# Normalising chunks 1 to 3 of x with channels on partitions, and sending the row statistics over ScalarE's queue

## The reference

```python
lat = layer_norm(_layernorm(x), ln_lat_g, ln_lat_b)
ctx = layer_norm(context, ln_ctx_g, ln_ctx_b)
q = (lat @ Wq)                      # 512 -> 1024
k, v = jnp.split(ctx @ Wkv, 2, axis=-1)
k = apply_rope(k, cos, sin)
attn = softmax(clip(q @ k.T * scale, -11, 11))       # 16 heads of 64
x = x + tanh(g_xattn) * ((attn @ v) @ Wo + bo)
x = x + tanh(g_ffn) * int8_product(_layernorm(x), rhs)
```

## Time and profile before

| | us |
|---|---|
| median of 3 runs | 1479.47 (1477.96 to 1479.47) |
| the profiled execution, its own time | 1478.47 |
| its span | 1476.7 |
| TensorE busy in it | 1444.3 |
| VectorE busy in it | 1268.0 |
| ScalarE busy in it | 705.0 |
| mean granted TensorE clock | 0.99 |

### The profile page before, as it was taken

How to read it: one execution, slowest core, us unless ns; L and a number is a source line. 1 busy time by engine, 2 the same in 40 slices (tenths; PEclk the granted TensorE clock), 3 DMA queues, 4 the chain that set the end, 5 groups by cost and what they waited for, 6 DMA issues and landing times. The chain is left out here.

```text
span 1476.7 us, 22445 instructions
## 1 busy us (share of the span) xinstructions
PE 1444.3 (98%) x7938; PEld 872.4 (59%) x7938; DVE 1268.0 (86%) x1112; ACT 705.0 (48%) x821; POOL 101.8 (7%) x66
## 2 busy tenths in 40 slices
PE   8988999999999999999999999999999999999997
PEld 7866888888887444444444444444444444444774
DVE  6746878778774999999999999999999999996987
ACT  4422222222232665665656556565565656654342
POOL 0400000000000000000000000000000000001775
PEclk9998999999999999999999999999999999999998
DMA  8786777677667445541551551551452452403552
GB/s 278 262 240 234 258 261 225 223 249 239 242 196 248 113 102 185 137 109 44 136 127 26 135 128 32 133 127 38 122 128 47 111 128 56 103 16 94 156 165 86
DMA packets 156992, 219.22 MB, mean 148 GB/s; under 512 B 39697, under 2 KB 89873, under 8 KB 149777
## 3 DMA queue, kind: packets, MB, share of 16 engines
q1 hardware_dynamic: 153792, 213.35, 49.4%
q10 hardware_dynamic: 3152, 5.25, 1.0%
HBM read 133.70 MB, written 84.84 MB: 148 GB/s over the span
## 5 line engine op out<-in xcount | busy, mean ns | idle before, releaser
L1158 ACT ACTIVATE prob<-score_ps 128x1024 f32<-128x1024 f32 x512 | 483.0, 1032 | 198.7 <-PE score_ps L1105 198.7
L1117 PE MATMUL value_ps<-prob,v_st 128*64 128x512 f32 x2048 | 467.7, 598 | 1.0 <-DVE prob L1200 1.0
L1216 DVE TENSOR_TENSOR prob_sum<-prob_sum,prob 128x2048 f32<-128x2048 f32 x192 | 440.1, 2292 | 13.5
L1105 PE MATMUL score_ps<-q_st,k_st 64*128 64x512 f32 x3072 | 394.5, 402 | 2.2 <-PEq L112 2.1
L1105 PEld LDWEIGHTS score_ps<-q_st,k_st 64*128 64x128 f32 x3072 | 271.3, 184 | 173.7 <-issue 105.6
L1200 DVE TENSOR_SCALAR prob<-prob 128x4096 f32<-128x4096 f32 x128 | 292.6, 2286 | 41.3 <-ACT prob L1158 39.1
L1117 PEld LDWEIGHTS value_ps<-prob,v_st 128*64 128x64 f32 x2048 | 135.6, 136 | 267.6 <-issue 265.4
L873 DVE TENSOR_TENSOR k_cos<-k_raw,rope 128x1024 f32<-128x1024 f32 x32 | 39.2, 1224 | 64.3 <-ACT k_raw L702 64.3
L1525 POOL MEMSET unround<- 128x1 f32 x1 | 0.1, 98 | 1281.7 <-POOLq L122 1281.7
L702 ACT ACTIVATE k_raw<-proj_ps 128x1024 f32<-128x1024 f32 x31 | 31.9, 1029 | 111.9 <-PE proj_ps L245 111.9
L711 ACT ACTIVATE v_out<-proj_ps 128x1024 f32<-128x1024 f32 x31 | 31.9, 1030 | 110.5 <-PE proj_ps L245 110.5
(11 more groups left out here) (125 smaller groups left out, 1320.3 us busy)
## 6 DMA issues: line engine op xcount, KB each, us to landing
k_st<-k_scr SPq DMA_DIRECT2D x128, 256.0 KB, 6.2
k_scr<-k_hi SPq DMA_DIRECT2D x64, 256.0 KB, 2.9
v_scr<-v_out SPq DMA_DIRECT2D x32, 512.0 KB, 3.8
k_scr<-k_lo SPq DMA_DIRECT2D x64, 256.0 KB, 4.4
q_st<-q_scr SPq DMA_DIRECT2D x16, 1024.0 KB, 10.6
v_st<-v_scr SPq DMA_DIRECT2D x16, 1024.0 KB, 13.5
q_scr<-q_hi SPq DMA_DIRECT2D x32, 256.0 KB, 5.2
q_scr<-q_lo SPq DMA_DIRECT2D x32, 256.0 KB, 4.7
```

Source lines behind the costliest of these rows:

```text
L1105: last = pe.matmul(score_ps[:, u % BANKS, a, :], k_st[slot][rows, k_part, s * P:(s + 1) * P], q_st[slot][rows, q_part, cols], start=(t == ...
L1117: last = pe.matmul(value_ps[rows, :], v_st[slot][:, s, rows], prob[:, b % 2, i, a * CH:(a + 1) * CH], start=(s == 0), stop=(s == STEPS - 1))
L1158: act.activation(prob[:, b % 2, u % BATCH_UNITS, :], score_ps[:, u % BANKS, :, :], ACT.Exp, scale=SCALE).then_inc(exped, 1)
L1216: dve.tensor_tensor(total, total, halves[j], ALU.add).then_inc(added, 1)
```

## The change

Chunks 1 to 3 of x are now prepared like the context. A second copy of x with channels on partitions, `x_t`, is an input. Each of these chunks is loaded as rows for the statistics and from `x_t` as columns (`load_columns`) into storage that is free at the time: `k_lo` for chunks 1 and 3, `rope` for chunk 2. The transposes of these chunks, the normalisation of rows and the affine step out of `turn_ps` are gone; chunk 0 keeps them.

The statistics of chunks 1 to 3 and of context chunk 0 no longer go over SyncE. ScalarE stores them after its copy of m = 1 (`store_stats`), and after its copy of m = 2 it waits for the landing and issues the two broadcasts (`spread_stats`). During chunk n, all for chunk n + 1 (context chunk 0 counts as chunk 4): ScalarE takes the root after m = 0 and applies gain and bias after m = 4; VectorE inverts after m = 0, normalises after m = 3, splits after m = 5, and measures the chunk after that one after m = 7. `split_weight` stays at m = 4 and m = 6, behind the affine step. The scales of `rhs` are stored and loaded back by ScalarE, at (2, 4) and (2, 5).

From context chunk 1 on, only names and counts change. The core of the diff:

```diff
+    qtok = [rope[:, :, :, :].rearrange("p s f c -> p (s f) c"),
+            k_lo[:, :, :, :].bitcast(F32).rearrange("p s h c -> p (s h) c")]
+    def columns(n, slot):
+        return qtok[slot] if isinstance(n, int) and n < QCH else ctok[slot]
+    def loads(n, slot):
+        return n // 2 + slot
...
-        def load_chunk(n, slot, src):
-            if n >= 2:
-                sp.wait_ge(turned, KT * (n - 1))
-            sp.dma_start(raw[:, slot, :, :], src.rearrange("(t p) d -> p t d", p=P)).then_inc(raw_in[slot], 16)
-        def load_rows(c, tok0):
...
-                sp.wait_ge(ctx_moments_made, c)
-            sp.dma_start(raw[:, 0, :, :], context[bass.ds(tok0, CH), :].rearrange("(p t) d -> p t d", t=CT)
-                         ).then_inc(raw_in[0], 16)
-        def load_columns(c, slot, tok0):
-            if isinstance(c, int) and c < 2:
+        def load_rows(n, src, tok0):
+            slot = 1 if isinstance(n, int) and n == 1 else 0
+            if isinstance(n, int) and n == 2:
+                sp.wait_ge(turned, KT)
+            elif not (isinstance(n, int) and n == 1):
+                sp.wait_ge(moments_made, n - 1)
+            sp.dma_start(raw[:, slot, :, :], src[bass.ds(tok0, CH), :].rearrange("(p t) d -> p t d", t=CT)
+                         ).then_inc(raw_in[slot], 16)
+        def load_columns(n, slot, src, tok0):
+            if isinstance(n, int) and QCH <= n < QCH + 2:
                 sp.wait_ge(wkv_lo_made, KT)
-            else:
-                sp.wait_ge(tok_lo_made, QCH + c - 1)
-            sp.dma_start(ctok[slot], context_t[bass.ds(tok0, DIM), :].rearrange("(k p) c -> p k c", p=P)
+            elif not (isinstance(n, int) and n < 3):
+                sp.wait_ge(tok_lo_made, n - 1)
+            sp.dma_start(columns(n, slot), src[bass.ds(tok0, DIM), :].rearrange("(k p) c -> p k c", p=P)
                          ).then_inc(ctok_in[slot], 16)
...
-        def spread_stats(c, slot, row):
-            sp.wait_ge(ctx_rstd_made, c + 1)
+        def spread_stats(n, slot, row):
+            sp.wait_ge(rstd_made, n)
             sp.dma_start(stat_scr[bass.ds(row, 2), :].rearrange("f (p t) -> p f t", t=CT), stat[:, slot, :, :]).then_inc(stat_stored, 16)
-            sp.wait_ge(stat_stored, 16 * (c + 1))
-            if isinstance(c, int) and c == 0:
-                sp.wait_ge(tok_lo_made, QCH)
+            sp.wait_ge(stat_stored, 16 * n)
...
         def load_rope(c, slot, s0):
-            if not isinstance(c, int) or c >= 2:
+            if isinstance(c, int) and c < 2:
+                sp.wait_ge(tok_lo_made, 3)
...
-        def store_scales():
-            sp.wait_ge(rhs_inv_made, 1)
-            sp.dma_start(ready.scale_scr.rearrange("f (p t) -> p f t", t=KT), rhs_scales[:, :, :]
-                         ).then_inc(ready.scale_stored, 16)
-        def load_inverses():
-            sp.wait_ge(ready.scale_stored, 16)
-            sp.dma_start(inv_row[:, :], ready.scale_scr[1:2, :].broadcast_to((P, DIM))).then_inc(inv_row_in, 16)
         def load_piece(i, wo_row, rhs_row):
 
             if isinstance(i, int) and i == 0:
-                sp.wait_ge(turned, KT * QCH)
+                sp.wait_ge(moments_made, 1)
...
-        load_chunk(1, 1, chunk_rows(1))
+        load_rows(1, x, CH)
+        load_columns(1, 1, x_t, CH)
...
-                if m == 0 and n + 2 < QCH:
-                    load_chunk(n + 2, n % 2, chunk_rows(n + 2))
-                if m == 0 and n + 2 >= QCH:
-                    load_rows(n + 2 - QCH, (n + 2 - QCH) * CH)
+                if m == 0:
+                    load_rows(n + 2, *((x, (n + 2) * CH) if n + 2 < QCH else (context, (n + 2 - QCH) * CH)))
+                if (n, m) in ((0, 3), (1, 0)):
+                    load_columns(n + 2, n, x_t, (n + 2) * DIM)
                 if (n, m) in ((2, 5), (3, 1)):
-                    load_columns(n - 2, n - 2, (n - 2) * CH)
+                    load_columns(n + 2, n - 2, context_t, (n - 2) * DIM)
                 if (n, m) in ((0, 3), (1, 0), (1, 4), (2, 0)):
                     load_rhs_column((0, 1, 3)[n] + (m == 4))
-                if (n, m) == (2, 7):
-                    spread_stats(0, 0, 0)
-                if (n, m) == (2, 4):
-                    store_scales()
-                if (n, m) == (2, 6):
-                    load_inverses()
...
+        def sqrt(n, slot):
             twice = isinstance(n, int) and n < QCH
-            act.wait_ge(meanvar_made, turns_before(n, part) + 1)
-            act.activation(std[:, tiles], meanvar[:, tiles, 1], ACT.Sqrt, bias=(eps_sq if twice else eps_col)[:, 0:1],
+            act.wait_ge(meanvar_made, n)
+            act.activation(std[:, :], stat[:, slot, 1, :], ACT.Sqrt, bias=(eps_sq if twice else eps_col)[:, 0:1],
                            scale=1.0 + EPS if twice else 1.0).then_inc(std_made, 1)
...
+        def affine(n, slot):
             which = 0 if isinstance(n, int) and n < QCH else 2
-            if not isinstance(n, int) or n >= 1:
-                act.wait_ge(tok_lo_made, n)
+            tile = columns(n, slot)
+            act.wait_ge(scaled, n)
             for k in range(KT):
-                act.wait_ge(turned, KT * n + k + 1)
-                act.activation(tok[:, k, :], turn_ps[:, k, :], ACT.Identity, bias=gains[:, which + 1, k:k + 1],
+                act.activation(tile[:, k, :], tile[:, k, :], ACT.Identity, bias=gains[:, which + 1, k:k + 1],
                                scale=gains[:, which, k:k + 1]).then_inc(affine_made, 1)
 
-        def sqrt_rows(c, slot):
-            act.wait_ge(ctx_aggregated, c + 1)
-            act.activation(std[:, :], stat[:, slot, 1, :], ACT.Sqrt, bias=eps_col[:, 0:1]).then_inc(ctx_std_made, 1)
-        def affine_columns(c, slot):
-            act.wait_ge(scaled, c + 1)
-            for k in range(KT):
-                act.activation(ctok[slot][:, k, :], ctok[slot][:, k, :], ACT.Identity, bias=gains[:, 3, k:k + 1],
-                               scale=gains[:, 2, k:k + 1]).then_inc(affine_made, 1)
+        def store_scales():
+            act.wait_ge(rhs_inv_made, 1)
+            act.dma_start(ready.scale_scr.rearrange("f (p t) -> p f t", t=KT), rhs_scales[:, :, :]
+                          ).then_inc(ready.scale_stored, 16)
+        def load_inverses():
+            act.wait_ge(ready.scale_stored, 16)
+            act.dma_start(inv_row[:, :], ready.scale_scr[1:2, :].broadcast_to((P, DIM))).then_inc(inv_row_in, 16)
+        def store_stats(n):
+            act.wait_ge(rstd_made, n)
+            act.dma_start(stat_scr[2 * n:2 * n + 2, :].rearrange("f (p t) -> p f t", t=CT), stat[:, n % 2, :, :]
+                          ).then_inc(stat_stored, 16)
+        def spread_stats(n):
+            act.wait_ge(stat_stored, 16 * n)
+            act.wait_ge(tok_lo_made, 1)
+            for f in range(2):
+                act.dma_start(rows[:, n % 2, f, :], stat_scr[2 * n + f:2 * n + f + 1, :].broadcast_to((P, CH))
+                              ).then_inc(rows_in[n % 2], 16)
...
-                if (n, m) == (0, 0):
-                    sqrt(1)
-                if m == 6 and n + 2 < QCH:
-                    sqrt(n + 2)
-                if m == 6 and n + 2 == QCH:
-                    sqrt_rows(0, 0)
-                if m == (4 if n == 0 else 3) and n + 1 < QCH:
-                    affine(n + 1)
-                if m == 3 and n + 1 == QCH:
-                    affine_columns(0, 0)
-                if m == 5 and n + 1 == QCH:
+                if m == 0:
+                    sqrt(n + 1, (n + 1) % 2)
+                if m == 1:
+                    store_stats(n + 1)
+                if m == 2:
+                    spread_stats(n + 1)
+                if m == 4:
+                    affine(n + 1, (n + 1) % 2)
+                if (n, m) == (2, 4):
+                    store_scales()
+                if (n, m) == (2, 5):
+                    load_inverses()
+                if (n, m) == (3, 5):
                     wo_high(0)
...
-        def measure_rows(c, slot):
-            dve.wait_ge(raw_in[0], 16 * (c + QCH // 2))
-            for t in range(CT):
-                last = dve.bn_stats(moments[:, t, :], raw[:, 0, t, :])
-            last.then_inc(ctx_moments_made, 1)
-            if not (isinstance(c, int) and c < 2):
-                dve.wait_ge(stat_stored, 16 * (c - 1))
-            dve.wait_ge(ctx_moments_made, c + 1)
+            if not (isinstance(n, int) and n < 3):
+                dve.wait_ge(stat_stored, 16 * (n - 2))
+            dve.wait_ge(moments_made, n)
             dve.memset(spacer[:, :], 0.0)
             for t in range(CT):
                 last = dve.bn_aggr(stat[:, slot, :, t], moments[:, t, :])
-            last.then_inc(ctx_aggregated, 1)
...
-        def invert_rows(c, slot):
-            dve.wait_ge(ctx_std_made, c + 1)
-            dve.reciprocal(stat[:, slot, 1, :], std[:, :]).then_inc(ctx_rstd_made, 1)
-        def normalise_columns(c, slot):
+            last.then_inc(meanvar_made, 1)
```

(90 more changed lines are left out.)

71 lines of the change are left out of this document (30 added, 41 removed).

## The result

The changed kernel takes 1521.59 us (median of 5 runs, 1520.55 to 1523.66) against 1478.87 before: a ratio of 1.0296, with an interval from 1.0282 to 1.0309. It is 43 us slower. I had forecast 1501 in a range of 1485 to 1518. The profiled execution took 1523.66 us, its span is 1521.8.

What follows compares the result with a forecast made beforehand. TensorE, busy 98% of the span, was taken as the bound: new stops 36.6 and clock 8.6, less 22.6 won, make 22.4 us on the profiled 1478.5, so 1501 us, range 1485 to 1518.

Steps and rivals of the forecast that it cites:

- The 22.6 us to be won: Ceiling on TensorE: 17.3 us from stops of 8.68 and 3.94 with slow groups, 5.3 from three sets of transposes.
- N: Start of VectorE's subtraction for the next chunk; TensorE can start that chunk at N + 10.1, or N + 19.9 if held twice.
- GpSimd's hold: Chunks 0 and 1: GpSimd's 4.64 us subtractions delay VectorE's two casts twice, N + 19.9 in place of N + 11.9; chance 0.5.
- Rival 1: GpSimd holds VectorE's casts once, not twice: 4.64 us less in each of two chunks, 1492 us; not held, 1485; chance 0.22.
- The row at 41.27: Old kernel's VectorE: one L746 TENSOR_SCALAR took 4.92 us, median 0.54, over GpSimd's subtraction; taken as the hold's price.
- the column of rhs in chunk 1: Issued about 61.3, landing 72.2, ahead of VectorE's normalising; N = 73.5, a 17.0 us stop, VectorE's wait near 9.
- The trip: Statistics from ScalarE's store to VectorE's first use: 8.8 us, 3.0 for the store and 5.8 for the broadcasts.
- I take 3.0 us: Landing time assumed for the statistics' 4 KB store on ScalarE's queue; bounds 3.0 and 8.2 us.
- rival 2: ScalarE's queue gives no shorter trip, 14.1 us stays; 19 us more, 1520; chance 0.15.
- the extra loads: 3 MB of x_t and 1.5 MB of broadcasts, 12 us of DMA time at 379 GB/s, priced at nothing.
- the clock: TensorE's slow first group after a stop: 2.6 us after each long stop, 1.7 after each short one, 8.6 together.
- the mark: When TensorE is full again in the context's first product: 129.45 us before, forecast 151.9, 22.4 us more.

Runs made afterwards that it cites:

- run 1: The changed kernel with GpSimd made to wait for VectorE's tok_lo before its low parts of the k and v weights: 1505.97 us.
- run 2: The changed kernel with its 1 MB loads issued behind the statistics' round trip, rows after m = 4 and columns after m = 5: 1511.0 us.
- run 3: The changed kernel with the statistics stored and spread by SyncE again, behind its stores of m = 1, in place of ScalarE: 1526.51 us.
- run 4: The kernel before, with only the statistics of context chunk 0 stored and spread by ScalarE in place of SyncE: 1477.04 us, ratio 0.9999.
- Run 5: The changed kernel plus an unneeded 2 MB store on SyncE at (2, 0), 0.1 us ahead of the statistics: 1523.41 us in one run.

## Why the prediction was right and wrong

**Right: the sign, the place and the number of stops.** The 22.6 us to be won were won (the two old stops with their slow groups, and the transposes) and are outweighed by one stop per chunk. After the start of the subtraction, N, the chain is as worked out: N + 19.6 in chunk 0 (36.14 to 55.71, forecast 19.9), N + 19.5 in chunk 1 (77.04 to 96.58), N + 10.1 in chunk 2 (117.33 to 127.47, forecast 10.1).

**Right: GpSimd's hold, twice in each of two chunks.** Casts of 8.92 and 8.91 us in place of 1.28; run 1 takes it away and wins 15.6 us, 14.3 of them in these two stops. Rival 1, held once, is refuted. The row at 41.27 was not quite the one exception before: GpSimd's other subtraction there, at 36.01, took 5.67 us in place of 4.64 beside `tok_lo` (34.88 to 37.17), which also reads two operands from SBUF.

**Right: the column of rhs in chunk 1.** It landed in 10.2 us and held VectorE 8.06, forecast 10.9 and near 9. The stop there, 16.39, was forecast as 17.0. The trip, 13.3 us at most, lay under it, but only just, as run 2 shows; so a part of this hit is luck. Two small errors cancel as well: SyncE issued the column 9.95 us after the chunk's start where I had 9.2 (and the items that I named for it add up to 7.9 only), and it landed 0.7 sooner than forecast.

**Wrong: "I take 3.0 us, the later stores' value, since ScalarE's queue holds little else".** This is the step that failed. The store took 7.0, 6.7 and 9.6 us in chunks 0, 2 and 3, and the trip was not 8.8 but 12.8, 12.6 and 19.9 us. The 5.8 us of the broadcasts held in chunks 0 and 2 (5.8 and 6.0) and failed in chunk 3 alone (10.2, from 145.13 to 155.34). That is my rival 2, to which I gave 0.15: the queue gives no shorter trip. Runs 3, 4 and 5 show it: on SyncE's queue the trips are hardly longer or shorter, the queue alone gains nothing, and 2 MB more on the other queue make the trip 5.4 us longer. That the rival's 1520 comes within 1.6 us of the median is luck in part: it had 14.1 us for each trip, two were shorter and one was 5.8 longer, and it did not have the `q_lo` below.

The row that spoke for the rival stood in my own list: 8.2 us for 4 KB at 93.48. The 3.0 came from the context stage, and I did not ask what the DMA share is there: 0.55 over such a trip, and 0.76 over the one at 93.48. Nor is the share enough to price it: in chunk 1 of the changed kernel the store landed after 3.1 us at a share of 0.93, while only 129 GB/s moved; in the other three chunks it was 288 to 301 GB/s. And I did not see what runs 3 and 4 show, that SyncE, freed of the wait, sends its next 1 MB into the trip: 19.9 us for 13.4, and 17.9 for 14.1.

The Trainium skill ("DMA: Bandwidth & Descriptors", the section on issuing engines that are not separate DMA queues) says that transfers run on the same 16 engines and interleave, whoever issues them, and that only issuing time is saved. Runs 3 and 4 agree (4.9 us more, and a ratio of 0.9999). Run 5 agrees in that the other queue's 2 MB count, but the 4 KB landed 1 us behind them.

**Costed at nothing: the extra loads. Not shown to be wrong.** I wrote that they were 12 us of DMA time, and "without the stops as cover they would lengthen the trips". The engines were full in the trips: over the four of the changed kernel the windows view has a DMA share of 0.99, 0.92, 0.97 and 0.97. But little of that is `x_t`. Its first load had landed at 19.0 us, ahead of all trips; the second was issued at 33.85, 2.3 us before the trip of chunk 0 ended; the third, at 65.18, lies in chunk 1, where it was counted with the column. In the trips of chunks 2 and 3 there are rows and columns of the context, tables and stores of q, which the kernel before moves as well. What is new is where they lie. Run 2 moves all 1 MB loads, old and new, and so doesn't tell the extra ones apart.

**Missed: what the context's first product waits for.** Its row says `q_lo`, not `tok_hi`. VectorE makes the `q_lo` of m = 6 behind `tok_lo` (165.37 and 167.57 above), so the stop ends at N + 13.2 (155.34 to 168.51) and not at N + 10.1: 3.1 us more.

**Mis-sized: the clock.** I had 1.7 us for each of two stops of 3.15, and they became 6.50 and 16.75. Also the shorter of them was followed by a slow group of 5.1 us; the four groups cost 9.5 in place of 8.6.

The account, measured less forecast: chunk 0 3.2 (16.55 for 13.3), chunk 1 -0.6, chunk 2 3.3, chunk 3 13.6 (16.75 for 3.15: the trip 11.1, `q_lo` 3.1, and 0.6 less elsewhere), clock 0.9. That is 20.4 of the 21.7 us by which the mark lies later than forecast (173.54 for 151.9); the rest is a late start of 0.2 and small pauses at the stops. For chunk 3, run 3 gives a part of the answer to what made the trip long: with nothing issued behind the store until 154.35 it took 13.4 us, 7.6 for the store and 5.8 for the broadcasts, so the traffic issued behind it is worth up to 6.5 of the 19.9. Run 5 varies what is ahead. How the engines order the two is not settled.

## What to carry to other kernels

A round trip through memory for a few KB took 9 to 20 us here, by what the DMA engines had to move meanwhile, whatever queue issued it. Take its price from a stretch where as many bytes are under way, and not from the share alone; start it ahead of the next large load, and see what the engine that used to wait for it will issue instead. When work moves within a hand-written order, look for what the other engines do at its new place: here GpSimd's subtractions had cost TensorE nothing for as long as no cast lay beside them. Replacing 5.3 us of transposes on the full engine by a chain over three engines and the memory pays only if the whole chain fits into the time between two chunks.

## What the runs showed of the hardware

Two things beyond what I had expected. A store of 4 KB, alone on ScalarE's queue, landed after 3.1 us in one chunk and after 9.6 in another of the same kernel, and after 13.7 us with 2 MB issued 0.1 us ahead of it on SyncE's queue, 1 us behind those. And GpSimd came in between two casts in all eight pairs of casts that met its subtractions (8.91 to 8.93 us in place of 1.28, in the changed kernel and in runs 2, 3 and 5): issuing two casts back to back kept none of them from waiting for a whole GpSimd instruction.
